# Expert layers of the last stage: gates as broadcast rows, experts in pairs, one accumulation a tile

## The reference

```
h  = relu(x @ sW1 + sb1);  h = relu(h @ sW2 + sb2);  shared = h @ sW3 + sb3
p  = softmax(x @ gW + gb);  the two largest are kept, and softmax again gives gate[node, e]
g1 = relu(x @ eW1[e] + eb1[e])       256 -> 128
g2 = relu(g1 @ eW2[e] + eb2[e])      128 -> 64
o  = g2 @ eW3[e] + eb3[e]             64 -> 256
out = residual + shared + sum over e of gate[node, e] * o[e]
```

## Time and profile before

| | us |
|---|---|
| three timed runs | 5016.27, 5008.64, 5015.13 |
| their median | 5015.13 |
| the profiled execution | 5005.29 |
| its span in the profile | 5003.6 |

### The profile page before, as it was taken

How to read it: one execution, slowest core, us unless ns; L and a number is a source line. 1 busy time by engine, 2 the same in 40 slices (tenths; PEclk the granted TensorE clock), 3 DMA queues, 4 the chain that set the end, 5 groups by cost and what they waited for, 6 DMA issues and landing times. The chain is left out here.

```text
span 5003.6 us, 88968 instructions
## 1 busy us (share of the span) xinstructions
PE 4472.9 (89%) x33844; PEld 4080.3 (82%) x33844; DVE 3161.3 (63%) x2662; ACT 2812.2 (56%) x3797; POOL 1399.1 (28%) x1058
## 2 busy tenths in 40 slices
PE   3556899999998599867999999989999999799989
PEld 3444679999998599834899999978999999688755
DVE  6994428888885411154688888817888887355323
ACT  1661337777775233322477877726788777244332
POOL 0000002222221122200166666612666666000000
PEclk9788899999998799978999999999999999899989
DMA  3882114333431555421334344323434442644000
GB/s 88 137 138 38 46 26 101 89 101 89 101 95 32 185 181 181 143 58 41 76 98 108 96 109 101 92 66 91 108 97 105 101 109 72 156 117 113 17 17 21
DMA packets 198455, 467.88 MB, mean 94 GB/s; under 512 B 107412, under 2 KB 145054, under 8 KB 176119
## 3 DMA queue, kind: packets, MB, share of 16 engines
q1 hardware_dynamic: 180704, 432.06, 34.0%
q0 software_dynamic: 14016, 28.15, 2.3%
q10 hardware_dynamic: 3399, 2.76, 0.2%
HBM read 390.03 MB, written 72.83 MB: 93 GB/s over the span
## 5 line engine op out<-in xcount | busy, mean ns | idle before, releaser
L1161 PE MATMUL g2a_pso<-HX,g2a_wt 125*125 125x129 f32 x5000 | 603.3, 274 | 7.1 <-DVEq L1008 3.8
L1161 PE MATMUL g1a_pso<-HX,g1a_wt 125*125 125x129 f32 x5000 | 603.3, 274 | 4.8 <-ACT g1a_wt L1045 3.3
L1161 PE MATMUL g0a_pso<-HX,g0a_wt 125*125 125x65 f32 x5000 | 585.3, 271 | 4.8 <-ACT g0a_wt L1045 3.3
L1161 PEld LDWEIGHTS g2a_pso<-HX,g2a_wt 125*125 125x125 f32 x5000 | 576.8, 189 | 7.6 <-DVEq L1008 4.1
L1161 PEld LDWEIGHTS g1a_pso<-HX,g1a_wt 125*125 125x125 f32 x5000 | 576.9, 189 | 5.2 <-ACT g1a_wt L1045 3.5
L1161 PEld LDWEIGHTS g0a_pso<-HX,g0a_wt 125*125 125x125 f32 x5000 | 575.1, 190 | 5.3 <-ACT g0a_wt L1045 3.4
L1045 ACT ACTIVATE g0a_wt<-g0a_pst 125x1000 f32<-125x1000 f32 (+1 forms) x300 | 312.0, 1040 | 186.9 <-PE g0a_pst L1148 186.8
L978 DVE SCALAR_TENSOR_TENSOR g1a_x<-g1a_als,g1a_cd,g1a_as 125x3125 f32<-125x3125 f32 x100 | 358.6, 3586 | 82.4 <-PE g1a_pst L1148 72.3
L978 DVE SCALAR_TENSOR_TENSOR g2a_x<-g2a_als,g2a_cd,g2a_as 125x3125 f32<-125x3125 f32 x100 | 358.6, 3586 | 82.1 <-PE g2a_pst L1148 72.1
L1045 ACT ACTIVATE g1a_wt<-g1a_pst 125x1000 f32<-125x1000 f32 (+1 forms) x300 | 312.2, 1041 | 169.8 <-PE g1a_pst L1148 169.8
L978 DVE SCALAR_TENSOR_TENSOR g0a_x<-g0a_als,g0a_cd,HX 125x3125 f32<-125x3125 f32 x100 | 347.5, 3475 | 95.0 <-PE g0a_pst L1148 85.8
(11 more groups left out here) (495 smaller groups left out, 7999.1 us busy)
## 6 DMA issues: line engine op xcount, KB each, us to landing
g0a_nl<-lowered SPq DMA_DIRECT2D x50, 1367.2 KB
g1a_nl<-lowered SPq DMA_DIRECT2D x50, 1367.2 KB
g2a_nl<-lowered SPq DMA_DIRECT2D x50, 1367.2 KB
moe_wa<-in_L_ffn_W SPq DMA_DIRECT2D x56, 1024.0 KB, 4.8
lowered<-counts_nl SPq DMA_DIRECT2D x25, 1367.2 KB
g3a_nl<-lowered SPq DMA_DIRECT2D x25, 1367.2 KB
g0a_nl<-lowered SPq DMA_DIRECT2D x50, 158.7 KB
g1a_nl<-lowered SPq DMA_DIRECT2D x50, 158.7 KB
```

Of the source, the lines that this page charges most:

```text
L1161: last = nc.tensor.matmul(pso[0:R, unit(q, 0, k) % 2, 0:F + 1], wt[:, side, j * R:(j + 1) * R], HX[:, a, q * HG + k % HG, :], start=(a == ...
```

## The change

Four things change in the last stage.

1. Two experts' second layers are put side by side on the 128 output partitions. Each e2 is widened with zeros to 128 columns (the first of a pair in the left half, the second in the right), and two matmuls accumulate into one PSUM buffer. A pair is one entry of `layers`; there are 9 entries and 18 jobs a group. A memset on POOL and four small loads fill e2.
2. The gates are multiplied into the ReLU outputs of the pair (g2), and not into the third layer's results. For this the transposed gates in gT are written to DRAM (`gate_rows`) and read back as GB, each gate's row broadcast over the 64 partitions of its expert. GB lies in ROWS (printed as HX), a tile that is free by then. Both go in two pieces: columns 0 to 999 once two of the seven turns are copied, and the other 2125 at the end. DVE's `weight(j)` multiplies four halves of a group in place, 128x313.
3. The third layer is one accumulation a tile: w3, the biases, pair 0, pair 1, four matmuls into one buffer, and DVE adds once (`add(t)`). A step of the interleaving is now one matmul. YS is 20.
4. Ahead of group 0, the second exponential stands before job 6, PE waits for the gates at job 9, and the turns follow jobs 9 to 15. PE waits for `weighted` ahead of a group's first product; DVE weights group j + 1 between the additions of tiles 3 and 4 of group j.

```diff
-def stage_last_ffn(nc, m, a, xT, PR, X, OUT):
-    E = 4
+def stage_last_ffn(nc, m, a, xT, PR, X, OUT, GB):
+    E, PAIRS_ = 4, 2
     with Stage(nc, "ffn") as s:
-        e1, e2, e3 = s.sb("e1", [P, E, 2, P]), s.sb("e2", [P, E, 64]), s.sb("e3", [64, E, D])
-        b1, b2, c1, c2 = s.sb("b1", [P, 2]), s.sb("b2", [P, 1]), s.sb("c1", [P, E]), s.sb("c2", [64, E])
+        e1, e2, e3 = s.sb("e1", [P, E, 2, P]), s.sb("e2", [P, E, P]), s.sb("e3", [P, PAIRS_, D])
+        b1, b2, c1, c2 = s.sb("b1", [P, 2]), s.sb("b2", [P, 1]), s.sb("c1", [P, E]), s.sb("c2", [P, PAIRS_])
-        g1, g2 = s.sb("g1", [P, E, GROUP]), s.sb("g2", [64, 2, E, GROUP])
+        g1, g2 = s.sb("g1", [P, E, GROUP]), s.sb("g2", [P, 2, PAIRS_, GROUP])
+        blank, weighted, gates_out = s.sem("blank"), s.sem("weighted"), s.sem("gates_out")
+        gates_in = [s.sem(f"gates_in{n}") for n in range(2)]
...
-            layers.append((P, [w1[:, c, o * P:(o + 1) * P] for c in range(2)], xin, (h1, o, False), b1[:, o:o + 1]))
+            layers.append(([w1[:, c, o * P:(o + 1) * P] for c in range(2)], xin, (h1, o, False), b1[:, o:o + 1]))
         for e in range(E):
-            layers.append((P, [e1[:, e, c, :] for c in range(2)], xin, (g1, e, False), c1[:, e:e + 1]))
-        layers.append((P, [w2[:, c, :] for c in range(2)], [(h1, 0), (h1, 1)], (h2, None, True), b2[:, 0:1]))
-        for e in range(E):
-            layers.append((64, [e2[:, e, :]], [(g1, e)], (g2, e, True), c2[:, e:e + 1]))
+            layers.append(([e1[:, e, c, :] for c in range(2)], xin, (g1, e, False), c1[:, e:e + 1]))
+        layers.append(([w2[:, c, :] for c in range(2)], [(h1, 0), (h1, 1)], (h2, None, True), b2[:, 0:1]))
+        FIRST_GATED = 2 * len(layers)
+        for x in range(PAIRS_):
+            layers.append(([e2[:, 2 * x + o, :] for o in range(2)], [(g1, 2 * x + o) for o in range(2)], (g2, x, True), c2[:, x:x + 1]))
         JOBS_ = 2 * len(layers)
-        YS = U * (E + 1)
+        GATED = JOBS_ - FIRST_GATED
+        PARTS = 2 + PAIRS_
+        YS = U * PARTS
         GROUPS_ = T // U
-        FIRST_TURN = JOBS_ - len(FOURS) - 1
+        SECOND_EXP, FIRST_TURN = 6, 9
+        EARLY = (FOURS[1][-1] + 1) * R
...
-            late = [(w2[:], a["L1_ffn_sW2"].rearrange("(c p) n -> p c n", p=P)), (b2[:], a["c_sb2"]),
-                    (e2[:], a["L1_ffn_eW2"].rearrange("e p n -> p e n")), (c2[:], a["c_eb2"]), (w3[:], a["L1_ffn_sW3"]),
-                    (e3[:], a["L1_ffn_eW3"].rearrange("e p n -> p e n")), (b3[0:E, :], a["L1_ffn_eb3"]), (b3[E:E + 1, :], a["L1_ffn_sb3"].unsqueeze(0))]
+            late = [(w2[:], a["L1_ffn_sW2"].rearrange("(c p) n -> p c n", p=P)), (b2[:], a["c_sb2"]), (c2[:], a["c_eb2"]),
+                    (w3[:], a["L1_ffn_sW3"]), (e3[:], a["L1_ffn_eW3"].rearrange("(x o) p n -> (o p) x n", o=2)),
+                    (b3[0:E, :], a["L1_ffn_eb3"]), (b3[E:E + 1, :], a["L1_ffn_sb3"].unsqueeze(0))]
             for dst, src in late:
                 sp.dma_start(dst, src).then_inc(late_in, 16)
+            sp.wait_ge(blank, 1)
+            for e in range(E):
+                sp.dma_start(e2[:, e, (e % 2) * 64:(e % 2) * 64 + 64], a["L1_ffn_eW2"][e]).then_inc(late_in, 16)
+            for n, (moved, n0, n1) in enumerate(((2, 0, EARLY), (len(FOURS), EARLY, N))):
+                sp.wait_ge(gate_moved, moved)
+                sp.dma_start(m.GT[:, n0:n1], gT[0:E, n0:n1]).then_inc(gates_out, 16)
+                sp.wait_ge(gates_out, 16 * (n + 1))
+                for o in range(2):
+                    sp.dma_start(GB[o * 64:(o + 1) * 64, :, n0:n1],
+                                 m.GT.rearrange("(x o) n -> o x n", o=2)[o][:, n0:n1].partition_broadcast(64)).then_inc(gates_in[n], 16)
             for t in range(T):
                 sp.wait_ge(rows_done, t + 1)
                 tile_dma(sp, OUT[t * R:(t + 1) * R], X[:, t, :], stored)
         @block.gpsimd
         def _(pool):
+            nc.gpsimd.memset(e2[:], 0.0).then_inc(blank, 1)
             nc.gpsimd.memset(gT[:], 1.0).then_inc(ones_set, 1)
...
-                    last = nc.tensor.matmul(psh[0:rows, job % 4, 0:c1 - c0], lhs, x, start=(c == 0), stop=(c == len(left) - 1))
+                    last = nc.tensor.matmul(psh[:, job % 4, 0:c1 - c0], lhs, x, start=(c == 0), stop=(c == len(left) - 1))
                 last.then_inc(h_full, 1)
             def product(j, n):
-                k, y = divmod(n, E + 1)
-                t, at = j * U + k, j * YS + n
+                k, y = divmod(n, PARTS)
+                t = j * U + k
                 if n == 0:
                     pe.wait_ge(h_ready, (j + 1) * JOBS_)
-                if at > 2:
-                    pe.wait_ge(y_free, at - 2)
-                to = psy[0:R, at % 3, 0:D]
-                if y == 0:
-                    nc.tensor.matmul(to, h2[:, j % 2, k * R:(k + 1) * R], w3[:], start=True, stop=False)
-                    last = nc.tensor.matmul(to, gT[:, t * R:(t + 1) * R], b3[:], start=False, stop=True)
-                else:
-                    last = nc.tensor.matmul(to, g2[:, j % 2, y - 1, k * R:(k + 1) * R], e3[:, y - 1, :], start=True, stop=True)
-                last.then_inc(y_full, 1)
+                    pe.wait_ge(weighted, (j + 1) * GATED)
+                if y == 0 and t > 2:
+                    pe.wait_ge(y_free, t - 2)
+                to, at = psy[0:R, t % 3, 0:D], slice(k * R, (k + 1) * R)
+                left, right = ((h2[:, j % 2, at], w3[:]), (gT[:, t * R:(t + 1) * R], b3[:]),
+                               (g2[:, j % 2, 0, at], e3[:, 0, :]), (g2[:, j % 2, 1, at], e3[:, 1, :]))[y]
+                last = nc.tensor.matmul(to, left, right, start=(y == 0), stop=(y == PARTS - 1))
+                if y == PARTS - 1:
+                    last.then_inc(y_full, 1)
...
                 if n == 2 * (2 + E):
-                    pe.wait_ge(late_in, 16 * 8)
+                    pe.wait_ge(late_in, 16 * 11)
                 if n == FIRST_TURN:
                     pe.wait_ge(gates_ready, 1)
                 layer(0, n)
...
                 if ring and j > 1:
-                    act.wait_ge(y_full, (j - 1) * YS)
+                    act.wait_ge(y_full, (j - 1) * U)
...
-                if n == 2 * (2 + E):
-                    act.wait_ge(late_in, 16 * 8)
+                if n == SECOND_EXP:
                     gm.exponential(act, 1)
                     act.wait_ge(ones_set, 1)
+                if n == 2 * (2 + E):
+                    act.wait_ge(late_in, 16 * 11)
                 evacuate(0, n)
...
+            def weight(j):
+                for n in range(GATED):
+                    x, (c0, c1) = n // 2, half(n % 2)
+                    dve.wait_ge(h_ready, j * JOBS_ + FIRST_GATED + n + 1)
+                    to = g2[:, j % 2, x, c0:c1]
+                    nc.vector.tensor_tensor(to, to, GB[:, x, j * GROUP + c0:j * GROUP + c1], ALU.mult).then_inc(weighted, 1)
+            def add(t):
+                dve.wait_ge(y_full, t + 1)
+                nc.vector.tensor_tensor(X[:, t, :], X[:, t, :], psy[0:R, t % 3, 0:D], ALU.add).then_inc(y_free, 1)
+                nc.vector.drain().then_inc(rows_done, 1)
             gm.compute(dve)
             nc.vector.drain().then_inc(gates_ready, 1)
-            for t in range(T):
-                for y in range(E + 1):
-                    at = t * (E + 1) + y
-                    dve.wait_ge(y_full, at + 1)
-                    ps = psy[0:R, at % 3, 0:D]
-                    if y == 0:
-                        nc.vector.tensor_tensor(X[:, t, :], X[:, t, :], ps, ALU.add).then_inc(y_free, 1)
-                    else:
-                        nc.vector.scalar_tensor_tensor(out=X[:, t, :], in0=ps, scalar=GATE[:, y - 1, t:t + 1], in1=X[:, t, :],
-                                                       op0=ALU.mult, op1=ALU.add).then_inc(y_free, 1)
-                    nc.vector.drain()
-                nc.vector.drain().then_inc(rows_done, 1)
+            dve.wait_ge(gates_in[0], 32)
+            weight(0)
+            dve.wait_ge(gates_in[1], 32)
+            for j in range(GROUPS_):
+                for k in range(U):
+                    if k == 3 and j + 1 < GROUPS_:
+                        weight(j + 1)
+                    add(j * U + k)
...
+    m.GT = dram("gate_rows", [4, N])
...
-            stage_last_ffn(nc, m, a, XT, PR, X, out)
+            stage_last_ffn(nc, m, a, XT, PR, X, out, ROWS[:, 0:2 * N].rearrange("p (x n) -> p x n", x=2))
...
-    r["c_eb1"], r["c_eb2"] = g["L1_ffn_eb1"].T, g["L1_ffn_eb2"].T
+    r["c_eb1"], r["c_eb2"] = g["L1_ffn_eb1"].T, columns(g["L1_ffn_eb2"].reshape(-1))
```

6 lines of the change are left out of this document (3 added, 3 removed).

## The result

The changed kernel took 4954.27 us (median of 4 runs, 4947.72 to 4970.23), the kernel before 5011.89 us (median of 4, 5004.51 to 5016.27). The ratio is 0.9886, with a 95% interval of 0.9869 to 0.9903: 57.6 us less. Forecast were 4968.0 us and a range of 4957 to 4986. The sign is as forecast, and so is what happens inside the stage; the time lies 2.7 us under the range. A turn is here, as in the prediction, a change between kinds of matmul that costs g more on each side; a turn of the gates is something else, the transposes that fill gT.

A forecast was written before the change was run, and what follows sets the result against it. The prediction took PE's stream of matmuls to bound the last stage. Savings of 40.6 us (four groups), 5.3 (last group) and 1.2 (first group) sum to 47.1, which from the median of 5015.13 gives 4968.0 us; range 4957 to 4986.

The forecast's parts named there:

- What bounds the stage: Last stage: PE's stream of matmuls is the bound, busy for all 20 us from 4900 to 4920 at clock 1.00.
- L, p, g and the group: Interleaved groups: layer half L 1.051 us, product p 0.430, turn g 0.196; a group takes 29.48 instead of 39.63, 40.6 less.
- The last group as a whole: Last group, products alone: a tile costs 2.11 us instead of 3.167, 5.3 us less over five tiles.
- What a turn is: PE's stream: 0.196 us is paid where the matmul's row count falls in another class (128, 64 or 32 rows).
- A pair product followed by a layer: Interleaved groups: this step, which occurs nowhere in the trace before, was taken as free.
- The rival that every change of kind costs g: Every change between layer and product costs 0.196 us whatever the rows: 34.0 us a group, 4986 in all; chance 0.08.
- The start: First group: gates ready earlier, seven halves with a turn of the gates at 1.72 us each; 1.2 us less.
- The gate rows: DRAM write and broadcast at 388 GB/s: hidden, weighting done about 2.5 us before PE asks for it.
- The second piece: Gate rows' 2.18 MB broadcast: lands near 4834 to 4836, blocks DVE's first addition, with cover of 11 us.
- the rival: Gate rows come late, at 100 GB/s: PE waits, perhaps at lower clock, some 5 to 8 us, 4973 to 4976; chance 0.09.
- The base: Whole kernel: forecast counted from the median 5015.13 us; the profiled execution, 5005.29, lies 9.8 under it and would give 4958.2.
- the sum of 47.1: Last stage: total saving in us, 40.6 from four groups, 5.3 from the last group, 1.2 from the first.

The follow-up runs named there:

- the late version: The changed kernel with the first write of gate rows to DRAM waiting for all seven turns: 4941.89 us against 4931.76 for the change.

## Why the prediction was right, and where not

- **What bounds the stage**: right. In the groups PE had no idle time before and has none after, at a clock of 1.00.
- **L, p, g and the group**: right. 29.51 us for 29.48; the last group's tile 2.11 for 2.11. The last group as a whole gave 5.6 instead of 5.3. That DVE stood beside PE there, at 3.10 us a tile once the turns are gone, the prediction did not see; as the change removes four of DVE's five operations too, the number came out.
- **What a turn is**: right for this change, too narrow as a rule. Columns of 64 pay like rows of 64, 0.17 us. The Trainium skill, page "TensorEngine Tiling (Array Packing)", section "Key Properties", says that a change of the tiling mode drains TensorE. The rows agree for 5 and 64 rows and for 64 columns. The transposes with 4 stationary columns follow a layer of 128 columns without any surcharge (1.06 + 0.43 us, no more), so fewer columns than 128 don't always cost; which shapes count as another mode was read here from the rows alone.
- **A pair product followed by a layer**, the one step without a row of its own: free, as taken. The rival that every change of kind costs g would have given groups of 34.0 us and is refuted by the 29.51 and by the version with padded biases.
- **The start**: mis-sized. 1.2 us forecast, 2.8 measured. The term is the turn of the gates, taken at 1.72 us from a 64-column layer's surcharge (0.15 and 0.09 us) and measured at 1.48. With seven of them that is 1.7 us.
- **The gate rows**: hidden, as forecast, but by less. The transfer rate was mis-sized, 204 to 246 GB/s for 388: a row of mixed loads was taken for a broadcast. The cover of 1.9 us was real, and what a breach costs is the 8.6 us of the late version, of which some 4 are clock. The second piece came 1.7 us later than forecast, behind a cover of 8.7 us. The prediction gave the rival 5 to 8 us, with a shorter wait of 2 to 3.
- **The base**: this is the step that failed and put the time outside the range. The prediction says "against the median the forecast is 4968.0" and that the range "takes in both", the median and the profiled execution. It set its low end 1 us under what a run like the profiled one would give, as if the unchanged 4790 us could be no faster in the next runs than in that one. The runs show that they vary: by 15 us with the clock in one stage, on one chip, for either kernel, and the four runs of the first measurement of the change are 22.5 us apart, the lowest 10.6 us under the profiled one. From 4968.0 down to 4954.27 are 13.7 us: 3.2 as the median of before itself came out lower with a fourth run, 1.8 from the stage, 8.7 from the stages that nobody changed. What made just these 8.7 us stays open. On the same chip and with the groups kept apart, the gain is 48.9 us, 1.8 over the sum of 47.1.

## What to carry to other kernels

Where PE is the bound, count the changes of matmul shape in its stream, and not only its matmuls: a small one (5 or 64 rows, or 64 columns) between full ones cost 0.17 to 0.2 us on either side here, and zeros up to 128 rows and columns removed that at no cost to PE (in the last group, where DVE stood beside it, padding alone gained 0.07 us a tile). When small stationaries can be stacked to a full one, the saved matmuls come on top. And if an edit is confined to one stage, compare that stage in the two profiles first, and give the range of the total the spread of all the stages that weren't touched, on both sides.
